# Turning 128-row tiles by DMA from SBUF to SBUF, in place of TensorE, in the projection and output stages of an attention kernel

## What is computed

```python
def ln(x, g): ...                                  # (x - mean) * rsqrt(var + eps) * g
xn = ln(x, g_norm)
q  = (xn @ Wq).reshape(b, n, 16, 64)               # 16 heads
kv = xn @ Wkv                                      # one k and one v of 64 columns
q, k = l2norm(q) * q_scale, l2norm(k) * k_scale
sim  = einsum('bhid,bjd->bhij', q, k) * 8 + rel_pos_bias(n)    # a small network over 2n-1 positions
sim  = causal(sim), with one null key and value in front
out  = einsum('bhij,bjd->bhid', softmax(sim), v)
z    = ln(out @ Wout, g_out)
s    = 127 / max(abs(z))                           # per row
y    = clip(round(z * s), -128, 127) / s @ ternary.T + bias
return x + y
```

## Time and profile before

| | before |
|---|---|
| median of 3 runs | 1697.08 us |
| profiled execution: its time, its span | 1696.54 us, 1694.7 us |
| busy: PE, DVE, POOL, ACT | 93%, 79%, 76%, 71% of the span |
| mean granted TensorE clock | 0.982 of full speed |
| projection of batch 0, steady steps | about 160 to 260 us |
| attention of batch 0 | about 276 to 787 us |
| output of batch 0, then projection of batch 1 | about 787 to 1055 us |
| output of batch 1 | about 1567 us to the end |

### The profile page before, as it was taken

The page is one execution under the profiler, slowest core; times in us unless marked ns, Lnnn a source line. Parts: engine busy times, 40 slices in busy tenths (PEclk is TensorE's granted clock), DMA queues, the critical chain, the costliest instruction groups (busy, mean ns, idle before and its releaser), DMA issues.

```text
span 1694.7 us, 42246 instructions
## 1 busy us (share of the span) xinstructions
PE 1578.9 (93%) x15105; PEld 1073.8 (63%) x15124; DVE 1342.5 (79%) x2391; ACT 1195.8 (71%) x2232; POOL 1281.8 (76%) x891
## 2 busy tenths in 40 slices
PE   4888996999999999998999996999999999998998
PEld 2445554767777777775555554677777777776554
DVE  4457886898898888885888886888888888887687
ACT  4665775778778778777444776787787787788442
POOL 4662345999999999996553443999999999999453
PEclk9999997999999999998999997999999999999999
DMA  6001102111111101200122102012111111110022
GB/s 196 1 13 29 39 14 50 39 27 39 39 26 39 45 19 39 50 3 13 45 81 89 49 26 50 19 34 51 26 31 47 26 36 41 26 26 14 20 76 94
DMA packets 41309, 68.93 MB, mean 41 GB/s; under 512 B 8880, under 2 KB 9392, under 8 KB 41136
## 3 DMA queue, kind: packets, MB, share of 16 engines
q1 hardware_dynamic: 36544, 58.27, 14.0%
q10 hardware_dynamic: 4608, 8.39, 1.3%
HBM read 58.11 MB, written 8.54 MB: 39 GB/s over the span
## 4 chain that ended last, share of the span: by engine, by line
PE 63%; DVE 16%; issue 11%; ACT 3%; DVEq 1%; POOL 0%; ACTq 0%; DMA 0%; POOLq 0%
PE ps L1289 21%; PE ps L1262 11%; PE ps L1336 10%; PE ps L1265 10%; DVE work L1013 6%; PE ps L1226 4%; PE ps L1326 2%; PE ps L1239 2%; DVE ss L950 2%; DVE work L1041 1%; PE ps L1354 1%; DVE root_m L958 1%; DVE denom L1038 1%; DVE tab L937 1%; DVE stats L926 1%
## 5 line engine op out<-in xcount | busy, mean ns | idle before, releaser
L525 POOL TENSOR_TENSOR work<-work 128x1024 f16<-128x1024 f32 (+2 forms) x576 | 978.3, 1732 | 49.6 <-ACT work L684 46.9
L1013 DVE SCALAR_TENSOR_TENSOR work<-ps,tab 128x1024 f32<-128x1024 f32 (+3 forms) x640 | 669.1, 1060 | 146.2 <-PE ps L1265 139.2
L684 ACT ACTIVATE work<-work 128x1024 f32<-128x1024 f32 (+3 forms) x640 | 578.1, 924 | 207.8 <-DVE work L1013 202.8
L1289 PEld LDWEIGHTS ps<-vals,work 128*128 128x128 bf16 (+1 forms) x8704 | 545.3, 98 | 116.0 <-POOL work L525 2.7
L1289 PE MATMUL ps<-vals,work 128*128 128x129 f16 x8704 | 600.6, 221 | 2.0 <-POOL work L525 1.9
L1262 PE MATMUL ps<-qo,kT 128*128 128x512 f16 (+3 forms) x1280 | 344.1, 351 | 26.1 <-DVE work L1013 15.1
L1265 PE MATMUL ps<-qo,kT 128*128 128x512 f16 (+3 forms) x1280 | 342.3, 349 | 0.0
L1265 PEld LDWEIGHTS ps<-qo,kT 128*128 128x128 f16 x1280 | 123.1, 98 | 117.6 <-issue 3.3
L1226 PE MATMUL ps<-wq,tab 128*128 128x512 f16 x768 | 171.6, 380 | 4.2 <-DVE tab L943 4.0
L1336 PE MATMUL ps<-wout,work 128*128 128x512 f16 x768 | 174.8, 385 | 0.0
L740 ACT COPY work<-ps 128x1024 f16<-128x1024 f16 x64 | 61.7, 1015 | 112.5 <-PE ps L1326 112.5
(11 more groups left out here) (142 smaller groups left out, 1556.7 us busy)
## 6 DMA issues: line engine op xcount, KB each, us to landing
tab<-bias_table SPq DMA_DIRECT2D x64, 512.0 KB, 4.7
tab<-in_x SPq DMA_DIRECT2D x64, 256.0 KB, 2.6
out_x<-work ACTq DMA_DIRECT2D x32, 256.0 KB, 2.0
work<-in_L_cond_Wq SPq DMA_DIRECT2D x1, 2048.0 KB, 9.9
work<-in_L_cond_Wout SPq DMA_DIRECT2D x2, 1024.0 KB, 10.3
qo<-in_L_cond_w SPq DMA_DIRECT2D x1, 1024.0 KB, 7.4
qo<-in_L_cond_b SPq DMA_DIRECT2D x2, 256.0 KB, 5.5
qo<-in_L_cond_g SPq DMA_DIRECT2D x2, 256.0 KB, 6.5
```

Of the source, the lines that this page charges most:

```text
L525: pool.tensor_tensor(low[:, k % LRING, :, c0:512], probs[:, r, :, c0:512], high[:, r, :, c0:512], ALU.subtract).then_inc(low_pool, 1)
L684: act.activation(probs[:, k % RING, :, c0:512], probs[:, k % RING, :, c0:512], ACT.Exp).then_inc(expd, 1)
L1013: dve.scalar_tensor_tensor(out=probs[:, k % RING, :, c0:512], in0=ps[:, 2 * (k % 2):2 * (k % 2) + 2, c0:512], scalar=SCORE, in1=tab[:, :, ...
L1289: last = pe.matmul(ps[:, sum_bank(i, q), (t % SUMS) * VS:(t % SUMS + 1) * VS], parts[:, rings[part], e, s * P:(s + 1) * P], vals[:, j, :], ...
```

## The change

- The turns on PE (`b_turn_x`, the 16 blocks of q in `b_turn_q`, `c_turn`, `c_turn_y`) and the copies out of PSUM behind them on ACT (`b_turn`, `c_turn`, `c_yturn`) are gone. The 2 blocks of k are still turned on PE (`b_turn_k`).
- In their place SyncE issues DMAs that turn a tile from SBUF to SBUF: `turn_x` (256 KB, both float16 halves of x), `turn_q` (512 KB), `turn_o` (512 KB) and `turn_y` (128 KB), each with a semaphore for each of the two buffers.
- x is split before it is turned: ACT's `b_xhigh` (lag 1) casts the normalised tile from SBUF, and the low half moves from DVE (`b_xlow`, lag 2, reading PSUM) to POOL (`b_xlow`, lag 1, reading SBUF), between `b_low` and `b_power`. `xn` now lies in place of `x_in`, so `load_x` waits for the low half of tile t - 2.
- The projections use PSUM banks 0, 4 and 1, and wait once for the network's last use of these.

```diff
-P_BANK = (2, 3, 1)
+P_BANK = (0, 4, 1)
...
-        xn = carve(flat_tab, 2, D)
+        xn = x_in
+        xhl = carve(flat_tab, 2, D).bitcast(F16).rearrange("p u (a n) -> p u a n", a=2)
...
 # SyncE
                 def load_x(t, u):
-                    sp.wait_ge(b_xn, NT * b + t + 1)
+                    since(sp, b_xTl, NT * b + t - 1)
...
+                def turn_x(t, u):
+                    g = NT * b + t
+                    sp.wait_ge(b_xTl, g + 1)
+                    since(sp, b_proj, 3 * (g - 1) + 6)
+                    sp.dma_start_transpose(xT[:, u, :, :, :].rearrange("p a c r -> p (a c) r"),
+                                           xhl[:, u, :, :].rearrange("p a n -> p (a n)")).then_inc(b_xd[u], 16)
+
+                def turn_q(t, u):
+                    g = NT * b + t
...
+                    sp.wait_ge(b_lo, 2 * g + 1 + 4)
+                    sp.dma_start_transpose(qT[:, :, t * P:(t + 1) * P],
+                                           qhl[:, u, :, :].rearrange("p h w -> p (h w)")).then_inc(b_qd[u], 16)
...
-                return [(load_x, 0)], attend, [(reload_x, 3)]
+                def turn_o(t, u):
+                    g = NT * b + t
...
+                    sp.wait_ge(c_low, g + 1)
+                    sp.wait_ge(c_z, g + 1)
+                    sp.dma_start_transpose(oT[:, u, :, :, :].rearrange("p a c r -> p (a c) r"),
+                                           o_hl[:, u, :, :].rearrange("p a n -> p (a n)")).then_inc(c_Td[u], 16)
+
+                def turn_y(t, u):
+                    g = NT * b + t
+                    sp.wait_ge(c_yq, g + 1 + 1)
+                    sp.wait_ge(c_f, g + 1)
+                    sp.dma_start_transpose(yT[:, u, :, :], yq[:, u, :]).then_inc(c_yTd[u], 16)
+                return [(turn_q, 5), (turn_x, 1), (load_x, -1)], attend, [(turn_y, 4), (reload_x, 3), (turn_o, 0)]
...
 # GpSimd
-                project = [(b_low, 4), (b_power, 0)]
+                def b_xlow(t, u):
+                    pool.wait_ge(b_xTh, NT * b + t + 1)
+                    pool.tensor_tensor(xhl[:, u, 1, :], xn[:, u, :], xhl[:, u, 0, :], ALU.subtract).then_inc(b_xTl, 1)
+                project = [(b_low, 4), (b_xlow, 1), (b_power, 0)]
...
 # ScalarE
-                def b_xt(t, u):
...
+                def b_xhigh(t, u):
+                    g = NT * b + t
+                    act.wait_ge(b_xn, g + 1 + 2)
+                    since(act, b_xd[u], 16 * (g // 2))
+                    act.copy(xhl[:, u, 0, :], xn[:, u, :]).then_inc(b_xTh, 1)
...
-                project = [(b_q(0), 3), (b_q(1), 3), (b_xt, 2), (b_q(2), 3), (b_square, 3), (b_high, 4), (b_rootof, 3),
-                           (b_turn, 5)]
+                project = [(b_q(0), 3), (b_q(1), 3), (b_xhigh, 1), (b_q(2), 3), (b_square, 3), (b_high, 4), (b_rootof, 3)]
...
-                return project, attend, [(o_highs, 0), (store_last, 0), (c_turn, 1), (c_yturn, 4), (store, 7)]
+                return project, attend, [(o_highs, 0), (store_last, 0), (store, 7)]
...
 # VectorE
-                project = [(ones, 3), (b_unit, 4), (b_norm, 1), (b_values, 4), (b_xlow, 2), (b_turn, 5), (b_sum, 3),
+                project = [(ones, 3), (b_unit, 4), (b_norm, 1), (b_values, 4), (b_turn, 5), (b_sum, 3),
                            (b_stat, 0)]
...
 # TensorE
-                        pe.wait_ge(b_xTl, g + 1 + 1)
+                        pe.wait_ge(b_xd[u], 16 * (g // 2 + 1))
...
-                project = [(b_project(0, 1), 3), (b_turn_v, 4), (b_turn_x, 2), (b_project(2), 3), (b_turn_q, 5)]
+                project = [(b_project(0, 1), 3), (b_turn_v, 4), (b_project(2), 3), (b_turn_k, 5)]
...
+                    for u in range(2):
+                        pe.wait_ge(b_qd[u], 16 * (NT // 2) * (b + 1))
...
-                    pe.wait_ge(c_Tc, 2 * g + 2 + 1)
+                    pe.wait_ge(c_Td[u], 16 * (g // 2 + 1))
...
-                return project, attend, [(c_turn, 1), (c_turn_y, 4), (c_ternary, 5), (c_project, 2)]
+                return project, attend, [(c_ternary, 5), (c_project, 2)]
```

More of the change, by code:

```diff
@@ L326, in build @@
         low_dve, low_pool, b_vh, b_vl = (sem(n) for n in ("low_dve", "low_pool", "b_vh", "b_vl"))
-        c_high, c_low, c_T, c_Tc, c_z, c_st, c_mv, c_ve, c_rstd, c_zn, c_am, c_amx, c_rec, c_as, c_rs = (
-            sem(n) for n in ("c_high", "c_low", "c_T", "c_Tc", "c_z", "c_st", "c_mv", "c_ve", "c_rstd", "c_zn",
+        c_Td, c_yTd = ([sem(f"{n}{u}") for u in range(2)] for n in ("c_Td", "c_yTd"))
+        c_high, c_low, c_z, c_st, c_mv, c_ve, c_rstd, c_zn, c_am, c_amx, c_rec, c_as, c_rs = (
+            sem(n) for n in ("c_high", "c_low", "c_z", "c_st", "c_mv", "c_ve", "c_rstd", "c_zn",
                              "c_am", "c_amx", "c_rec", "c_as", "c_rs"))
-        c_y1, c_y2, c_yq, c_yT, c_yTc, c_f, c_xb, c_fin = (sem(n) for n in (
-            "c_y1", "c_y2", "c_yq", "c_yT", "c_yTc", "c_f", "c_xb", "c_fin"))
+        c_y1, c_y2, c_yq, c_f, c_xb, c_fin = (sem(n) for n in (
+            "c_y1", "c_y2", "c_yq", "c_f", "c_xb", "c_fin"))
         CB = 2 * NU
@@ L730, in o_highs @@
                 def o_highs(t, u):
[L731 removed]
+                    since(act, c_Td[u], 16 * ((NT * b + t) // 2))
                     act.copy(o_hl[:, u, 0, :].rearrange("p (h d) -> p h d", d=DH),
                              o_all[:, :, NT - 1 - t, :]).then_inc(c_high, 1)
[L735 to L748 removed]
                 def store(t, u):
@@ L1139, in _ @@
         def _(pe):
-            for s, n in ((b_xT, 2),
-                         (b_proj, 6), (b_vT, 2), (b_turned, 2), (pv_done, RING), (c_T, 2), (c_z, 2), (c_yT, 2), (c_f, 2)):
+            for s, n in ((b_proj, 6), (b_vT, 2), (b_turned, 2), (pv_done, RING), (c_z, 2), (c_f, 2)):
                 pe.sem_inc(s, n)
@@ L1199, in batch @@
             def batch(b):
-                def b_turn_x(t, u):
-                    g = NT * b + t
-                    pe.wait_ge(b_xn, g + 1 + 2)
-                    pe.wait_ge(b_xTl, g + 1)
-                    for c in range(KC):
-                        last = pe.transpose(ps[:, 0, c * P:(c + 1) * P], xn[:, u, c * P:(c + 1) * P],
-                                            ident[:, :])
-                    last.then_inc(b_xT, 1)
                 def b_project(*columns):
@@ L1219, in f @@
                             pe.wait_ge(b_qc, 3 * g + n + 1)
-                            if t == 0 and b and n < 2:
-                                pe.wait_ge(c_zn, NT * b - 1 + n + 2)
+                            if g == 0:
+                                pe.wait_ge(*((M[0]["Tc"], NT), (bias_row, NT - 1), (M[1]["Tc"], NT))[n])
                             for k, (rows, cols) in enumerate(PASSES):
@@ L1229, in b_project, with b_turn_k @@
                     return f
-                def b_turn_q(t, u):
+                def b_turn_k(t, u):
                     g = NT * b + t
                     pe.wait_ge(b_lo, 2 * g + 2 + 4)
-                    pe.wait_ge(b_ca, g + 1)
                     pe.wait_ge(b_cd, g + 1)
                     pe.wait_ge(b_vl, g + 1 + min(t + 2, NT) - t)
-                    for h in range(H):
-                        pe.transpose(ps[:, 4 + h // 8, :].bitcast(F16)[:, (h % 8) * P:(h % 8 + 1) * P],
-                                     qhl[:, u, h, :], ident16[:, :])
                     for a in range(2):
@@ L1318, in attend @@
                         weigh_slot(HP - 1, k)
-                def c_turn(t, u):
-                    g = NT * b + t
-                    pe.wait_ge(c_low, g + 1)
-                    pe.wait_ge(c_Tc, 2 * g + 1)
-                    for a in range(2):
-                        for c in range(2 * KC):
-                            last = pe.transpose(ps[:, a, :].bitcast(F16)[:, c * P:(c + 1) * P],
-                                                o_hl[:, u, a, c * P:(c + 1) * P], ident16[:, :])
-                    last.then_inc(c_T, 1)
                 def c_project(t, u):
                     g = NT * b + t
-                    pe.wait_ge(c_Tc, 2 * g + 2 + 1)
+                    pe.wait_ge(c_Td[u], 16 * (g // 2 + 1))
                     pe.wait_ge(c_zn, g + 1)
@@ L1338, in c_project @@
                     last.then_inc(c_z, 1)
-                def c_turn_y(t, u):
-                    g = NT * b + t
-                    pe.wait_ge(c_yq, g + 1 + 1)
-                    pe.wait_ge(c_yTc, g + 1)
-                    for c in range(KC):
-                        last = pe.transpose(ps[:, 4, 0:256].bitcast(BF16)[:, c * P:(c + 1) * P],
-                                            yq[:, u, c * P:(c + 1) * P], identb[:, :])
-                    last.then_inc(c_yT, 1)
                 def c_ternary(t, u):
                     g = NT * b + t
-                    pe.wait_ge(c_yTc, g + 1 + 1)
+                    pe.wait_ge(c_yTd[u], 16 * (g // 2 + 1))
                     pe.wait_ge(c_fin, g + 1)
```

57 lines of the change are left out of this document (16 added, 41 removed).

## The result

The changed kernel takes 1710.26 us (median of 5 runs, 1704.72 to 1715.99) against 1696.88 us (5 runs, 1695.62 to 1697.27) for the kernel before beside it: ratio 1.0076, 95% interval 1.0050 to 1.0103, so 13.4 us slower. The profiled execution is the slowest of the five: 1715.99 us, span 1714.1. What follows accounts for its span, which is 19.4 us above the 1694.7 of before.

A forecast was written before the change was run, and what follows sets the result against it. PE was taken to bound the output, and PE with a nearly equal loop the projection. From 1696.5 us, -24 (output), +32 (projection), +3 and +1.5 (exposed turns) gave 1709 us; whole range 1675 to 1980.

The forecast's parts named there:

- The projection step: Projection: a new loop through DVE, ACT and POOL sets 9.37 us a step against 8.13, 32 us more in both batches.
- GpSimd's hold on the quotient: Projection step: DVE's quotient (L963) waits for POOL's b_xlow to end, so it finishes 0.86 us late.
- rival 1: Projection: POOL does not hold up DVE, the loop is 8.51 us and the total 1687 us; chance 0.13.
- The output step: Output: DVE becomes the bound, the step falls from 7.16 to 6.37 us, 24 us gained in both batches.
- Sum: Whole kernel: 1696.5 - 24 + 32 + 3 + 1.5 = 1709 us.
- the start of attention: Last turn of q replaces PE's turn and a copy, table load behind it: -2.5 to +5 us, taken at nothing.
- The outputs' beginnings: First sums turn of each output: 4.7 us replaces PE turns (1.1) and two copies (about 2), +1.6 us each.
- The DMA turns: SBUF-to-SBUF turns cost what plain transfers do, 2.6 us for 256 KB and 4.7 for 512 KB, mostly hidden.
- the signs: Listed observations that would show the forecast right, among them turns landing in under 3 us (x) and 5 (q, sums).
- Rival 2: Projection and output: the DMA queue becomes the bound, 2378 us at 0.104 us a run, 1980 at 0.069; chance 0.26.
- Rival 3: Projection and output: PE's savings of 1.7 and 1.3 us a step come through in full, 1601 us; chance 0.01.
- the clock: PE's granted clock in the projection: expected 1.00, with about 6.0 of 9.4 us busy; named as a risk.

## Why the prediction was right

- **The projection step.** Forecast 9.37, measured 9.36 to 9.38. The mechanism was right, and part of the exactness is luck: in the step from 186.40 to 195.78 us the way from the low part to `b_norm` took 5.51 and not 5.39, the rest 3.87 and not 3.98. The term for GpSimd's hold on the quotient was 0.86 and measured 0.98, because `b_xlow` took 1.16 and not 1.04. The 8.13 for before was read over seven steps that take turns, four short and three long; it is 8.16. Moving `b_xlow` alone brought 8.25, 0.26 below the 8.51 that rival 1 gives for a loop without the hold: from the low part to `b_norm` it was 4.53 as worked out, the rest 3.72 and not 3.98, mostly because `b_norm` took 0.54 us there. By the Trainium skill, SBUF — State Buffer, under who interferes with whom, the loser of the shared port pair waits for the other's whole instruction. The 192 and 1167 ns agree with it.
- **The output step.** Forecast 6.37, measured 6.28; VectorE bound it (0.2 us of waits for PE in 1620 to 1690 us) and its wait for GpSimd's L597 stayed (1.57 us).
- **Sum.** 12.5 us forecast against 13.4 in the medians. That is closer than the terms were: they were worked out for a profiled execution, and between the two profiled executions it is 19.4, the changed one being the slowest of five that spread over 11 us. Of the 6.9 us that are missing, the start of attention, taken at nothing, has 5.3: the way to the first bias add is 1.3 and 2.0 us shorter, but behind it attention loses 3.9 and 4.7 us, because the second table load is late too and not the first alone (DVE waits 3.44 us for it in batch 0). The net 2.6 and 2.7 lie inside the bounds (-2.5 to +5). The projection of batch 0 has 1.1 (17.1 against 16), and the stretch with projection 1 has 2.0 when its start of attention is taken out; output 1 gives back 1.6 (-10.6 against -9).
- **The outputs' beginnings** were mis-sized, and it helped: the first DMA turn was to cost 1.6 us in each. From POOL's first low part to the first statistics it is 14.44 and 14.82 us, where it was 14.95 and 15.33, 0.5 less in each. Before, the first matmul of `c_project` came 5.65 us after the first turn on PE had begun (787.20, 792.85), not 3.1; with the change 4.4 us after the DMA's issue (806.98, 811.35).
- **The DMA turns.** From issue to landing (medians) x took 3.1 us, which is just over the "under 3" of the signs, q 4.5, the sums 5.1 and the quantised row 3.0; plain loads of 256 and 512 KB took 3.1 and 4.7. The plain transfers were the right row. By an estimate from the 261 GB/s of the Trainium skill, DMA: Bandwidth & Descriptors, section on latency and other measured facts, 512 KB would move in 2.0 us. Here 4.5 and 5.1 were measured; it changed little, as all but the first and last turns are hidden. The Trainium skill, VectorE: DVE Perf Modes, in its section on the three transpose paths, gives 1309 ns for one 128x128 block by DMA. Here 16 blocks took 4.5 us together, so it is no price per block.
- **Rival 2, the queue.** It would have decided at 0.049 and 0.040 us a run. From the queue's part of the windows, 55.4% x 80 x 16 / 28649 = 0.025 us a packet in the projection (164 to 244 us) and 75.4% x 90 x 16 / 37691 = 0.029 in the output (1610 to 1700): half and nearly three quarters of those. The second turn of the quantised row shows another limit, SyncE's time for its issues, which the rival did not have. The chance of 0.26 and the upper end of 1980 rested on the mean packet of 0.104, four times what a short one costs.
- **Rival 3** was excluded by VectorE's 6.28 and the loop, as forecast.
- **Wrong: the clock.** I expected 1.00 in the projection, and it was 0.87 to 0.94, with what follows for PE's waits, which were to be some 3 us in each step; see below.

## What to carry to other kernels

When work moves between engines, ask first which loop it closes and what it runs beside: here the place of one 1.16 us operation in a list decided over 27 to 28 us. Before crediting a new mechanism, give the old one the same order of work: 22 of the 27 us came from the order. Whether a DMA turn hides is a matter of what stands between its issue and its use. The 512 KB of the sums had one output step of 6.28 us for their 5.1, and VectorE did not wait; x with one projection step was waited for (22.8 us in all), with two it was not. Whatever stands behind a turn on the issuing engine is late by its wait and its issue too, and that engine can itself become full.
